# Keys and values of two batches instead of one behind the last expert tile

## The chip, the cores and the metric

The kernel runs on one core of a Trainium2 chip, as one program. A core has TensorE (matmuls), VectorE, ScalarE and GpSimd for everything elementwise, SyncE, which mostly starts transfers, and 16 DMA engines that all of them share. The metric is the device time of one execution in microseconds (us); lower is better. It is given as the median of several runs.

## The reference

The input x has 8 batches of 512 tokens with 256 channels, the context as many. Four residual steps follow each other:

```python
x = x + _L0_xattn_ref(_layernorm(x), ctx, ctx, ...)      # gated attention without softmax
x = x + _L0_ffn_ref(_layernorm(x), Ws, bs, W1, b1, W2, b2)
x = x + _L1_xattn_ref(_layernorm(x), ctx, ctx, mask, Wq, Wk, Wv, Wo)
x = x + _L1_ffn_ref(x, ...)                              # self attention, then top-2 experts
```

The second step is a mixture of experts in which each of 8 experts takes the 512 tokens with the highest router probability:

```python
route_prob = softmax(xf @ Ws + bs).T
route_vals, routes = top_k(route_prob, k)                # k = N / E = 512
h = gelu(einsum('ekd,edf->ekf', xf[routes], W1) + b1)
out = (einsum('ekf,efd->ekd', h, W2) + b2) * route_vals
final = zeros.at[routes].add(out)
```

The third step, a cross attention with 16 heads of 16 channels, needs `k = key @ Wk.T` and `v = value @ Wv.T`, where key and value are both the context. They do not depend on x, so they can be computed at any time before it. This case is about when.

## The kernel before, in words

The program is a row of blocks. In each block every engine has its own instruction stream, written out in program order; engines meet by semaphores, and at the end of a block by a barrier: each engine issues a DRAIN (which ends when its own work is over) and reports to GpSimd, and GpSimd lets all of them go when all have reported and its own DRAIN is over. In the rows below those instructions bear the line at which the block ends: 861 for the search block, 1365 for an experts' block, 1979 for the attention.

The blocks are: `aft_keys`, `aft_tokens` (first attention, router), `expert_choice` (here called the search block), `experts` for the first layer (the experts' block), `attention` (cross and self attention), `experts` for the second.

The **search block** finds, for each of 8 experts, the 512th highest probability by 15 rounds of bits. In a round VectorE compares and TensorE counts. Then token lists of the first two experts are made: VectorE builds one-hot slabs, TensorE sums them (line 701), VectorE enters the list, and GpSimd fetches the tokens' rows by eight indirect gathers (line 711, tile `early_xg`). TensorE is mostly free in this block, so the cross attention's keys and values are projected there, in units put between the rounds. A batch has four units:

```python
if q == 0: self.keys(pe, b, 0)
if q == 1: self.keys(pe, b, 1); self.take_off(pe, b, 0, 0, K0)
if q == 2: self.values(pe, b, 0); self.take_off(pe, b, 1, 0, K1); self.take_off(pe, b, 0, 1, MID0)
if q == 3: self.values(pe, b, 1); self.take_off(pe, b, 1, 1, MID1)
```

`keys` (line 754) and `values` (line 772) are fp32 matmuls. The keys are kept as three bf16 parts: ScalarE copies a bank out as bf16, `take_off` (line 761) subtracts that part in the bank by a matmul with minus one times the identity, and ScalarE copies the rest, twice. So a batch has eight ScalarE copies (`copy_batch`, lines 802 to 818). SyncE stores three parts of keys to `kstack` (line 823, 256 KB each) and the values to `values` (line 829, 574 KB), and loads the context of the batch after next (line 159). Batches count from 0 to 7; batch b uses buffer b % 2.

After the fourth list sum of the search block TensorE runs the units that are left: the last one of batch 5 and all of batch 6 before, with `B - LATE = 7` batches in this block.

The **experts' block** runs 8 tiles of 512 tokens. In a tile TensorE multiplies by W1 (line 1549), ScalarE applies the activation (line 1591), TensorE turns the next tile's rows (line 1537) and multiplies by W2 (line 1571), VectorE adds the bias and scales (lines 1699, 1703), and GpSimd adds the result to the tensor `sum` by indirect transfers with accumulation (line 1495), one at a time. Behind the last tile TensorE projects the batches that are left (batch 7 before), in the banks `exL_pt` and `exL_ph`. SyncE's stream there is:

```python
for b in range(B - LATE, B):
    kv.store_part(sp, G, b, 0, K1)
    kv.store_part(sp, G, b, 1, MID1)
    kv.store_values(sp, G, b)
    if b == B - 1:
        sp.wait_ge(added, begins(tiles) * 16)
        opening.load_rows(sp, G)
    kv.store_part(sp, G, b, 2, LO1)
```

`opening.load_rows` (line 1248) loads the first batch of the new x from `sum` once all scatter-adds are over. VectorE then takes its statistics (lines 370, 373), GpSimd makes the reciprocal spread (lines 380, 381), VectorE normalizes (line 386, tile `open_xn`), and the block ends. The attention starts with TensorE turning `open_xn` (line 2093).

Of the kernel before, what the change touches and what calls it, by code (L numbers as in the profile page):

```python
# [728 lines left out]
FIRST = 2  # L729
K0, K1, MID0, V0, MID1, LO0, V1, LO1 = range(8)  # L730
EVENTS = 8
LATE = 1


class KeyValues:
# [96 lines left out]
def expert_choice(nc, G, a, early, source):  # L832
# [4 lines left out]
    with ExitStack() as ctx:  # L837
# [16 lines left out]
            "vchain", "counted", "totalled", "flagged", "scanned", "ranked", "built", "summed"))  # L854
        kv = KeyValues(st, early, source, pk, pv, 0, B - LATE)
        entered, copied, masked = (st.sem(n) for n in ("entered", "copied", "masked"))
# [4 lines left out]
        with nc.Block() as block:  # L861

            @block.sync
            def _(sp):
                st.set_semaphores(sp)
                early.st.set_semaphores(sp)
                st.retire(sp, G["aft_sems"])
                st.retire(sp, G["tok_sems"])

                def load_expert(e):  # L870
                    sp.dma_start(early.w1[e][:], a["L0_W1"][e].rearrange("(c p) f -> p c f", p=P)).then_inc(early.w1_in[e], 16)
                    sp.dma_start(early.b1[e][:], a["L0_b1"][e]).then_inc(early.w1_in[e], 16)
                    sp.dma_start(early.w2[e][:], a["L0_W2"][e].rearrange("(c p) d -> p c d", p=P)).then_inc(early.w2_in[e], 16)
                    sp.dma_start(early.b2[e][:], a["L0_b2"][e:e + 1, :].broadcast_to([P, D])).then_inc(early.w2_in[e], 16)

                for e in range(FIRST):
                    load_expert(e)

                for b in range(B - LATE):
# [3 lines that stand above are left out]
                    if b + 2 < B:  # L883
                        source.load(sp, a, b + 2)
                    kv.store_part(sp, G, b, 2, LO1)

            @block.scalar
            def _(act):
                act.copy(onesb[:], G["ones"][:]).then_inc(copied, 1)
                act.activation(minus[:], G["identb"][:], ACT.Copy, scale=-1.0).then_inc(copied, 1)  # L890
                for b in range(B - LATE):
                    kv.copy_batch(act, b)
# [111 lines left out]
            def _(pe):  # L1004
                left = iter(range(4 * (B - LATE)))

# [263 lines left out]
def experts(nc, G, a, tag, gelu, early=None, out=None, opening=None, source=None):  # L1270
# [7 lines left out]
    with ExitStack() as ctx:  # L1278
# [32 lines left out]
        if early:  # L1311
            kv = KeyValues(st, early, source, pt, ph, B - LATE, B)
        names = ("turned", "xgT_ready", "hid_ps", "hid_ready", "out_ps", "ys_ready", "put_ready", "biased")
# [51 lines left out]
        with nc.Block() as block:  # L1365

            @block.sync
            def _(sp):
# [24 lines left out]
                if early:  # L1393
                    opening.st.set_semaphores(sp)
                    run(sp, load, 2)
                    opening.load_weights(sp, a)
                    for b in range(B - LATE, B):
                        kv.store_part(sp, G, b, 0, K1)
# [1434 lines left out]
```

## Time and profile before

| | |
|---|---|
| median of 3 runs | 2377.77 us (2376.32 to 2379.54) |
| profiled execution, its own time | 2372.58 us |
| span in that profile | 2370.4 us |
| mean granted TensorE clock | 0.963 |
| TensorE busy | 2177.3 us (92%) |
| VectorE busy | 1339.2 us (56%) |
| ScalarE busy | 1005.1 us (42%) |
| GpSimd busy | 661.2 us (28%) |

The profile is of one execution; its times count from the start of the span. Busy time leaves out DMA-issuing, semaphore and branch instructions. PE is TensorE, PEld its weight loads, DVE VectorE, ACT ScalarE, POOL GpSimd, SP SyncE; a q behind the name (POOLq, SPq) is that engine's sequencer, with DMA issues, waits and DRAINs. The search block lies at 187 to 270 us, the experts' block at 270 to 542 us.

### The profile page before, as it was taken

Reading aid. Unit: us, or ns where it says so; the run is one execution under the profiler, and the core shown is the slowest. Engines: PE = TensorE matmul, PEld = TensorE weight load, DVE = VectorE, ACT = ScalarE, POOL = GpSimd, SP = SyncE. Lnnn points to the kernel's source line nnn. Section 1 sums busy time; section 2 is a strip of 40 time slices with the busy share of each in tenths; the row PEclk is TensorE's granted clock in tenths of the full one; section 3 lists DMA queues with packets and bytes.
Section 4 is the critical chain, followed back from the end, with each engine's and each line's share of the span. In section 5 each row is a group of like instructions: output and inputs, shape, how many; then the busy total and the mean of one; then the engine's idle time right before and its main releaser. Section 6 shows DMA issues by size and latency. Waiting matters only on the chain. (4 is left out here: it accounts for less than half of the span.)

```text
span 2370.4 us, 33096 instructions
## 1 busy us (share of the span) xinstructions
PE 2177.3 (92%) x10807; PEld 1230.4 (52%) x10807; DVE 1339.2 (56%) x3625; ACT 1005.1 (42%) x1823; POOL 661.2 (28%) x671
## 2 busy tenths in 40 slices
PE   6898899985999999999999999999858999999995
PEld 2474566661333433334334343334337888888884
DVE  5556533214777777777777777877854541112125
ACT  2223322110656665665666656666512222222223
POOL 3210233333111001111124233344122343334343
PEclk9998999995999999999999999999968999999997
DMA  5426434435333332321343342443106666667684
GB/s 175 136 98 200 140 97 104 117 70 99 72 66 68 60 69 33 73 51 26 44 55 55 46 55 42 60 64 48 26 31 186 190 186 188 188 189 208 198 274 127
DMA packets 197559, 249.75 MB, mean 105 GB/s; under 512 B 26080, under 2 KB 175584, under 8 KB 195360
## 3 DMA queue, kind: packets, MB, share of 16 engines
q1 hardware_dynamic: 175808, 217.95, 36.6%
q0 software_dynamic: 20736, 29.15, 7.1%
q10 hardware_dynamic: 864, 0.79, 0.3%
q8 instruction: 77, 1.26, 0.2%
q14 instruction: 74, 0.61, 0.1%
HBM read 162.77 MB, written 46.52 MB: 88 GB/s over the span
## 5 line engine op out<-in xcount | busy, mean ns | idle before, releaser
L2343 ACT ACTIVATE att_prob<-att_ps 128x512 f32<-128x512 f32 x1024 | 594.5, 597 | 388.1 <-PE att_ps L2187 200.5
L2477 DVE CUSTOM_DVE_ANT_0 att_junk<-att_pm,bias 128x512 bf16<-128x512 f32 x512 | 343.6, 688 | 166.6 <-PE att_pm L2170 165.3
L2170 PE MATMUL att_pm<-att_kstack,att_qstack 96*128 96x512 bf16 x1024 | 399.4, 391 | 29.1 <-DMA att_qstack<-att_q 24.5
L2473 DVE TENSOR_REDUCE att_tops<-att_pm 128x1 f32<-128x512 f32 x512 | 340.1, 682 | 114.3 <-PE att_pm L2170 112.3
L2184 PE MATMUL att_ps<-att_qstack,att_kstack 99*128 99x512 bf16 x1024 | 390.7, 383 | 9.2 <-DMA att_qstack<-att_negT 4.9
L1591 ACT ACTIVATE exL_hid<-exL_ph,exL_b 128x256 f32<-128x256 f32 (+1 forms) x312 | 144.3, 463 | 390.6 <-PE exL_ph L1549 389.5
L1495 POOL DMA_INDIRECT sum<-exL_ys,exL_put x106 | 176.3, 1663 | 405.9 <-DVE exL_ys L1703 229.6
L1549 PE MATMUL exL_ph<-exL_xgT,exL_w 128*128 128x256 f32 (+1 forms) x1248 | 271.9, 375 | 8.3 <-issue 4.4
L2201 PE MATMUL att_po<-att_prob,att_vals 128*32 128x512 f32 x2048 | 275.4, 610 | 1.0 <-ACT att_prob L2343 1.0
L1571 PE MATMUL exL_po<-exL_w,exL_hid 128*128 128x256 f32 x1184 | 265.4, 382 | 6.0 <-ACT exL_hid L1591 4.0
L2170 PEld LDWEIGHTS att_pm<-att_kstack,att_qstack 96*128 96x128 bf16 x1024 | 100.9, 99 | 300.3 <-DVE att_tops L2477 99.3
L1549 PEld LDWEIGHTS exL_ph<-exL_xgT,exL_w 128*128 128x128 f32 x1248 | 221.3, 192 | 53.7 <-ACT exL_hid L1591 10.9
L1571 PEld LDWEIGHTS exL_po<-exL_w,exL_hid 128*128 128x128 f32 x1184 | 221.8, 190 | 42.7 <-ACT exL_hid L1591 9.8
L2187 PE MATMUL att_ps<-bias,identb 128*128 128x512 bf16 x512 | 194.8, 380 | 0.0
L2184 PEld LDWEIGHTS att_ps<-att_qstack,att_kstack 99*128 99x128 bf16 x1024 | 100.0, 98 | 149.8 <-ACT att_prob L2343 80.5
L1645 DVE COPY exL_xgT<-exL_pt 128x256 f32<-128x256 f32 (+2 forms) x96 | 40.0, 458 | 221.6 <-PE exL_pt L1537 221.4
L380 POOL TENSOR_SCALAR open_rstd<-open_mv 128x4 f32<-128x4 f32 x16 | 3.7, 229 | 495.3 <-DVE open_mv L2450 486.1
L1699 DVE TENSOR_TENSOR exL_ys<-exL_po,exL_b 128x256 f32<-128x256 f32 x74 | 31.4, 424 | 188.0 <-PE exL_po L1571 184.0
L1571 PE MATMUL exL_po<-early_w,exL_hid 128*128 128x256 f32 x512 | 113.6, 381 | 8.6 <-DVE exL_ys L1703 8.6
L1549 PE MATMUL exL_ph<-exL_xgT,early_w 128*128 128x512 f32 x256 | 115.0, 604 | 1.5 <-DVE exL_xgT L1645 1.5
L1591 ACT ACTIVATE exL_hid<-exL_ph,early_b 128x512 f32<-128x512 f32 x64 | 44.0, 687 | 153.6 <-PE exL_ph L1549 153.6
L1571 PEld LDWEIGHTS exL_po<-early_w,exL_hid 128*128 128x128 f32 x512 | 96.2, 190 | 23.8 <-DVE exL_ys L1703 11.1
(415 smaller groups left out, 2614.9 us busy)
## 6 DMA issues: line engine op xcount, KB each, us to landing
exL_w<-in_L_W SPq DMA_DIRECT2D x78, 1024.0 KB, 5.4
att_qstack<-att_q SPq DMA_DIRECT2D x186, 128.0 KB, 5.7
early_w<-in_L_W SPq DMA_DIRECT2D x16, 1024.0 KB, 5.4
att_kstack<-att_k SPq DMA_DIRECT2D x96, 128.0 KB, 4.6
att_kstack<-kstack SPq DMA_DIRECT2D x32, 256.0 KB, 5.0
kstack<-early_k SPq DMA_DIRECT2D x24, 256.0 KB, 4.2
exL_b<-in_L_b SPq DMA_DIRECT2D x39, 128.0 KB, 5.5
values<-early_vals SPq DMA_DIRECT2D x8, 574.0 KB, 3.7
```

Of the source, the lines that this page charges most:

```text
L1495: pool.indirect_dma_start(out=sums[0], out_offset=bass.IndirectOffsetOnAxis(ap=put[slot][:, c:c + 1], axis=0), in_=ys[slot][:, c, :], in_o ...
L1549: mm = pe.matmul(ph[f % 2][:, 0:n * P], w1[slot][:, m, f * P:(f + 1) * P], xgT[:, m, 0:n * P], start=m == 0, stop=m == DC - 1)
L1571: mm = pe.matmul(po[c % 2][:], hid[:, f, c * P:(c + 1) * P], w2[slot][:, f, :], start=f == 0, stop=f == FC - 1)
L1591: act.activation(hid[:, f, 0:n * P], ph[f % 2][:, 0:n * P], gelu, bias=b1[slot][:, f:f + 1]).then_inc(hid_ready, 1)
L1645: ins = dve.tensor_copy(xgT[:, m, 0:n * P], pt[m][:, 0:n * P])
L2170: pe.matmul(pm[i % TOPS][:], stack["q"][par][0:KR, h, t * P:(t + 1) * P], stack["k"][par][0:KR, h, :], start=True, stop=True).then_inc(s[" ...
L2184: mm = pe.matmul(ps[i % 2][:], stack["k"][par][0:KR + 3, h, kc * P:(kc + 1) * P], stack["q"][par][0:KR + 3, h, :], start=True, stop=me.self_)
L2187: mm = pe.matmul(ps[i % 2][:], G["identb"][:], G["bias"][1][:, kc, :], start=False, stop=True)
L2201: mm = pe.matmul(po[j * 32:j * 32 + 32, :], vals[par][:, kc, h * VW:h * VW + 32], prob[(i + j) % PROBS][:], start=kc == 0, stop=kc == CB - 1)
L2343: act.activation(prob[i % PROBS][:], ps[i % 2][:], ACT.Exp, scale=SCALE).then_inc(s["p_ready"], 1)
L2473: ins = dve.tensor_reduce(tops[g % 2][:, t, j:j + 1], pm[i % TOPS][:], AX.X, ALU.max)
L2477: ins = dve.tensor_tensor_reduce(junk[:, i % TOPS, :], pm[i % TOPS][:], G["bias"][0][:, t, :], 1.0, -BIG / 2, ALU.add, ALU.max, tops[g % 2 ...
```

## The change

The number of batches whose keys and values are projected behind the last expert tile goes from one to two. Every loop that splits the batches between the two blocks reads it, on TensorE (units), ScalarE (copies) and SyncE (stores); VectorE and GpSimd keep their streams.

```diff
 FIRST = 2
 K0, K1, MID0, V0, MID1, LO0, V1, LO1 = range(8)
 EVENTS = 8
-LATE = 1
+LATE = 2
```

On TensorE, at the end of the search block. `pick_pk` and `pick_pv` are the banks of keys and values; `early_k` are the saved bf16 parts.

```order
 L772 MATMUL pick_pv<-source_wv,source_src 128x256 x4
 L761 MATMUL pick_pk<-early_k,early_minus 128x512
-L754 MATMUL pick_pk<-source_src,source_wk 128x512 x4
-L761 MATMUL pick_pk<-early_k,early_minus 128x512
-L772 MATMUL pick_pv<-source_wv,source_src 128x256 x4
-L761 MATMUL pick_pk<-early_k,early_minus 128x512 x2
-L772 MATMUL pick_pv<-source_wv,source_src 128x256 x4
-L761 MATMUL pick_pk<-early_k,early_minus 128x512
 L861 UNCONDITIONAL_BRANCH
```

Batch 6 is gone from there: behind batch 5's last values comes the end of the block. At the end of the experts' block the same six rows are put between the last tile's line 1571 and batch 7, in the banks `exL_pt` and `exL_ph`.

On SyncE, at the end of the search block and at the end of the experts' block.

```order
 L829 DMA values<-early_vals 128x1148
 L159 DMA source_src<-in_ctxT 128x2x512
-L823 DMA kstack<-early_k 128x2x512 x3
-L829 DMA values<-early_vals 128x1148
 L823 DMA kstack<-early_k 128x2x512
 L861 UNCONDITIONAL_BRANCH
```

```order
 L823 DMA kstack<-early_k 128x2x512 x2
 L829 DMA values<-early_vals 128x1148
+L823 DMA kstack<-early_k 128x2x512 x3
+L829 DMA values<-early_vals 128x1148
 L1248 DMA x<-sum 128x4x256
 L823 DMA kstack<-early_k 128x2x512
```

Four stores left the first place and stand in the second, ahead of the load of x at line 1248. The context loads of line 159 all stay in the search block. On ScalarE the eight copies of lines 802 to 818 move in the same way. The order of GpSimd's and VectorE's instructions is the same in both kernels.

## Rows read from the trace of the kernel before

**Rows 1.** Timeline of PE, 258 to 275: start, us, engine, what, idle before.

```profile
259.14 0.38 PE L761 MATMUL pick_pk<-early_k,early_minus 128*128 128x512 bf16 x1
...
266.89 0.38 PE L761 MATMUL pick_pk<-early_k,early_minus 128*128 128x512 bf16 x1
270.21 1.35 PE L1537 MATMUL exL_pt<-ident,early_xg 128*128 128x128 f32 x8 [2.94 <-PEq L861]
```

**Rows 2.** Line 861, end of the search block: count, ns min/median/max, first and last start.

```profile
L861 POOLq EVENT_SEMAPHORE  x2: 17/17/17, 270.0 to 270.0; - x2
L861 POOLq DRAIN  x1: 10547/10547/10547, 259.4 to 259.4; - x1
...
L861 SPq DRAIN  x1: 122/122/122, 268.6 to 268.6; - x1
```

**Rows 3.** Timeline of POOL, 255 to 270.

```profile
263.54 0.95 POOL L711 DMA_INDIRECT early_xg<-rows,early_get  x1 [0.30 <-issue]
```

**Rows 4.** Timeline of POOL, 520 to 545.

```profile
535.36 1.05 POOL L381 TENSOR_TENSOR open_rstd<-open_rstd,mhalf 128x4 f32<-128x4 f32 x1
```

**Rows 5.** Line 1365, end of the experts' block, 520 to 545.

```profile
L1365 POOLq DRAIN  x1: 6397/6397/6397, 535.3 to 535.3; - x1
L1365 DVEq DRAIN  x1: 1295/1295/1295, 536.7 to 536.7; - x1
```

**Rows 6.** End of the attention: line 1979, and POOL's last instruction.

```profile
L1979 POOLq DRAIN  x1: 2452/2452/2452, 1760.5 to 1760.5; - x1
...
1760.55 2.35 POOL L2407 TENSOR_TENSOR x<-x,att_yn 128x1024 f32<-128x1024 f32 x1
```

**Rows 7.** Timeline of PE, 518 to 552.

```profile
526.49 0.38 PE L761 MATMUL exL_pt<-early_k,early_minus 128*128 128x512 bf16 x1
542.18 1.09 PE L2093 MATMUL att_pja<-ident,open_xn 128*128 128x128 f32 x4 [15.30 <-PEq L1365]
```

**Rows 8.** Timeline of ACT, 518 to 545.

```profile
526.69 0.59 ACT L816 COPY early_vals<-exL_ph 128x512 f32<-128x512 f32 x1 [0.59 <-PE exL_ph L772]
```

**Rows 9.** Timeline of SP, 518 to 534.

```profile
527.31 0.33 SPq L829 DMA_DIRECT2D values<-early_vals  x1
528.42 0.36 SPq L1248 DMA_DIRECT2D x<-sum  x1
```

**Rows 10.** Waits of SP, 520 to 545: total us, times, longest.

```profile
SPq L1365 <- PEq L1365: 8.0, 1, 8.0
...
SPq L1248 <- DMA sum<-exL_ys,exL_put: 0.8, 1, 0.8
```

**Rows 11.** Timeline of DVE, 518 to 542.

```profile
532.97 1.40 DVE L370 BATCH_NORM_STATS2 open_stats<-x 128x6 f32<-128x256 f32 x4 [12.92 <-DMA x<-sum]
...
536.51 1.38 DVE L386 TENSOR_SCALAR open_xn<-x,open_mv,open_rstd 128x256 f32<-128x256 f32 x4 [1.73 <-POOL open_rstd L381]
```

**Rows 12.** Stretches: busy us of each engine, PEclk, DMA share, GB/s.

```profile
core 0: us, PE busy (x) PEld busy (x) DVE busy (x) ACT busy (x) POOL busy (x), PEclk, DMA share, GB/s
188.00:192.00 4.00, 3.83 (x5) 1.77 (x6) 1.47 (x6) 0.01 (x1) 1.11 (x3) 0.50 0.00 0
192.00:196.00 4.00, 4.00 (x17) 2.44 (x17) 1.25 (x6) 1.65 (x3) 0.00 (x0) 0.96 0.78 266
263.00:267.00 4.00, 4.00 (x20) 3.14 (x18) 0.00 (x0) 2.62 (x5) 1.18 (x2) 1.00 1.02 341
273.00:277.00 4.00, 3.98 (x5) 1.85 (x6) 3.70 (x8) 0.17 (x1) 0.00 (x0) 0.50 0.00 0
277.00:281.00 4.00, 4.00 (x10) 1.64 (x9) 2.56 (x7) 1.44 (x3) 0.00 (x0) 0.92 0.02 4
534.00:542.00 8.00, 0.00 (x0) 0.00 (x0) 2.13 (x10) 0.00 (x0) 1.31 (x3) 0.50 0.00 0
```

**Rows 13.** Issue to landing: load of x (L1248), then the context loads (L159) at 225:270.

```profile
DMA to landing us min/median/max: 4.5/4.5/4.5
...
DMA to landing us min/median/max: 5.1/5.2/6.9
```

## The prediction

> **What bounds the kernel now.** I read in this order: the busy line of the table above, each engine's timeline around the two places that the constant touches, the lines on which a block of the program ends, SyncE's waits, and the granted clock in short stretches. TensorE is busy for 92% of the span, but one batch of keys and values is a few us of it; what counts is which wait ends last at the end of the search block (line 861) and at the end of the first experts' block (line 1365).
>
> The search block. TensorE ends batch 5 at 259.14 + 0.38 = 259.52, batch 6 at 266.89 + 0.38 = 267.27, and then has nothing until 270.21 [rows 1]. Batch 6 is therefore 267.27 - 259.52 = 7.75 us of TensorE. Who holds the block until 270.0? Every engine ends it with a DRAIN. TensorE's work is over at 267.27, SyncE's DRAIN at 268.6 + 0.12 = 268.7, and GpSimd's lasts from 259.4 for 10.547 us, to 269.9; its two semaphore events, which let all engines go, stand at 270.0 [rows 2]. GpSimd's last instruction, the eighth gather of token rows, was over at 263.54 + 0.95 = 264.49 [rows 3]. So its drain goes on for 5.4 us behind its last instruction, and outlasts SyncE by 1.2 us.
>
> The experts' block shows the same. GpSimd's last instruction ends at 535.36 + 1.05 = 536.41 [rows 4], its drain at 535.3 + 6.40 = 541.7, that of VectorE at 536.7 + 1.30 = 538.0 [rows 5]: 5.3 us behind GpSimd's last instruction and 3.7 us behind VectorE. This is also no matter of traffic, since the DMA share from 534 to 542 is 0.00 [rows 12]. In the block of the attention, where GpSimd issues no indirect DMA, its last instruction ends at 1760.55 + 2.35 = 1762.90 and its drain at 1760.5 + 2.45, together with it [rows 6]. The reader is to see a fixed tail of 5.3 to 5.4 us, counted from GpSimd's own last instruction, in the two blocks that this change touches.
>
> Behind the last tile TensorE projects batch 7 until 526.49 + 0.38 = 526.87 and then idles for 15.30 us [rows 7]. In that gap runs a chain. ScalarE saves the second half of the values (526.69, 0.59) [rows 8]; SyncE stores them at 527.31, waits for the last scatter-add, and loads the first rows of x at 528.42 [rows 9], a wait of 0.8 us [rows 10]; VectorE's statistics start when they have landed, at 532.97, after 12.92 us of idling, and its last pass starts at 536.51 when GpSimd has given the spread [rows 11]; then come the 5.3 us of drain. Attention's first transposes start at 542.18 [rows 7].
>
> **The front: what the removal gives.** It takes the matmuls of batch 6, 7.75 us, from TensorE, eight copies from ScalarE and four stores (three of 256 KB, one of 574 KB) from SyncE, all behind the last thing that GpSimd needs: the fourth list sum of the block. GpSimd's and VectorE's streams are the same, so the eighth gather still ends at 264.49 and the drain still ends 5.3 to 5.4 us later. What I take away was under that cover: gain 0 us, at most 0.1 from the drain being 5.3 and not 5.4. If the drain were not fixed and fell with the stores, the block could end as soon as the last gather is issued: 270.0 - 264.5 = 5.5 us. That end I keep for a rival.
>
> It also has a cost. TensorE now idles from 259.52 to 270.2, 10.7 us and not 2.9. Before, the clock is at 0.50 from 273 to 277 and at 0.92 from 277 to 281 [rows 12], so it came back at about 277.6, and the eight transposes at 270.21 took 1.35 us, most of them still at full clock [rows 1]. After the 15.3 us of idling at the other place, four such transposes took 1.09 [rows 7], so eight take about 1.09 x 2 = 2.2, less the pipelined overlap, some 1.9: +0.55 us, in front of VectorE's copy and the first tile's matmuls. When the clock comes back after that is open from both sides. At the search block's begin TensorE was busy for 3.83 us of 188 to 192, that is from 188.2, at 0.50, and had 0.96 over 192 to 196, so full clock from about 192.3, 4.2 us after the restart [rows 12]; counted so from 270.2 it would be back at 274.4, 3.2 us earlier than before, worth 1.6 us of work at double speed. Before it took 7.4 us from that restart (270.2 to 277.6), for TensorE stood idle between the transposes and the first long matmuls, as it will again; and if it returned as much later as it can earlier, 1.6 us would be lost. I take 0 for it, and +0.5 for the term (range -1.1 to +2.2).
>
> A rule of the Trainium skill speaks against this change here: the page "TensorE: Matmul & The Clock Gate", section "Part 1: The HAM clock gate", has the array fall to 1.2 GHz once it has been idle and return to 2.4 GHz after sustained work. By that rule the transposes start slow, as the row after 15.3 us of idling shows; without it the term would be 0 and the sum 7.3.
>
> **The back: what the addition costs.** The same 7.75 us of matmuls, eight copies and four stores now stand ahead of batch 7, in the block whose end had TensorE idle for 15.3 us. Idle as TensorE is there, the work is not free, because x's load stands in SyncE's queue behind the store of batch 7's values, and this waits for their copy. Batches follow each other without a stall: the banks and buffers that batch 7's first keys need were saved by then, as in the search block, where batch 6 followed batch 5 at once. All of batch 7 moves by 7.75 us: its values are stored at 527.31 + 7.75 = 535.06. The last scatter-add does not move (it hangs on the last tile alone and is over at 528.4), so the 0.8 us wait is gone, and what was hidden in it is all the cover there is. The store takes SyncE 0.33 us [rows 9], so x's load is issued at 535.4, which is 7.0 us later than 528.42.
>
> Then the landing. Before it took 4.5 us, issued 1.1 us behind the 574 KB of values; in the search block a load of the same 512 KB, issued right behind such a store, took 5.1 to 6.9, median 5.2 [rows 13]. With 4.5 VectorE starts 7.0 us later, with 5.2 it is 7.7. The truth lies between and I take 7.3. Batch 6's own stores are no queue in front of it: 1.34 MB per 7.75 us, against the 341 GB/s that 263 to 267 shows [rows 12], are done in half that time. Behind the landing nothing changes: statistics, spread, last pass and drain hang on each other. SyncE stood 8.0 us at the barrier [rows 10], and its last store moves by at most 7.75 with the barrier, so it stays 8 us early. The next stage's loads and clock start from the same gap of some 15 us of idling, so I give them nothing.
>
> On the load the skill has a rule in "Trainium Kernel Development and Optimization", section "Key Constraints": DMAs of all queues share the same 16 engines and interleave. By it the load pays for values' bytes still under way and lands nearer to the 5.2; with queues independent of one another it would be 4.5. Sum 7.7 or 7.0.
>
> **Sum.** Front: 0 gained, +0.5 lost at the clock. Back: +7.3. Together +7.8 us. The profiled execution took 2372.58 us, 2.2 more than its span of 2370.4; with the change it would be 2380.4. The median of the runs is 2377.77, 5.2 above the profiled one, so the predicted median is 2385.6, 0.33% slower. The terms' bounds give +7.0 - 1.1 = 5.9 to +7.7 + 2.2 = 9.9, so 2383.7 to 2387.7.
>
> **Rivals.**
> A. The drain is not fixed. Place: the end of the search block. If GpSimd's drain waits for transfers or for the other engines' traffic, removing batch 6 ends the block up to 5.5 us earlier, and the sum is +7.8 - 5.5 = +2.3, 2380.1 us: not slower by more than a measurement can tell (0.2%, 4.8 us, is the bound for that). It decides as soon as more than 3.0 of the 5.5 us come back. For it: the last gather was still in flight when the drain began, and the stores were too, with a DMA share of 1.02 [rows 12]. Against it: the drain of the second block was as long (5.3) with no byte moving. Chance 0.08.
> B. The back is hidden. If something else than batch 7's values held x's load, the second batch would be free: sum 0.5, 2378.3 us. For it: TensorE's 15 us of idling there, which look like room. Against it: SyncE waits 0.8 us for the scatter-add and no more. It would need a scatter-add that ends 7 us later than in this trace. Chance 0.04.
> C. The clock costs more than I give it: the return to full speed comes a whole step later in the first tile and the landing is at its upper end, +9.9 us, 2387.7. Same sign as the forecast. Chance 0.12.
> D. A real gain, by an effect that I do not see. Chance 0.02. My forecast keeps 0.74.
>
> From these: slower by over 0.2% has 0.74 + 0.12 = 0.86, less 0.01 for a forecast that falls just under the bound: 0.85; within 0.2%: A, B and that, 0.13; faster 0.02. The range takes in the terms' bounds and 1 us to each side for the spread of medians (the three runs span 3.2 us): 2382.6 to 2388.6. It leaves out A and B.
>
> **What would show it.** In the profile after: the search block's GpSimd drain ends again at about 269.9 with SyncE's now before 262; no batch 6 in that block, TensorE idle for 10.7 us; the eight transposes at 1.8 to 2.0 us; 15.6 us of projections behind the last tile; the wait for the scatter-add gone from SyncE's waits; x's load issued about 7 us later against the last scatter-add, and attention's first transpose some 7.8 us later than 542.18. I am wrong if the drain ends before 268 (A), if x's load is issued before 530 (B), or if the first tile's matmuls run at half clock beyond 281 (C).

## The result and the profile after

The change makes the kernel slower: 2385.27 us against 2377.77 us, medians of 7 runs each, ratio 1.003 with a 95% interval of 1.0017 to 1.0043. 1.003 is 7.1 us, the interval 4.0 to 10.2 us. The forecast was +7.8 us, to 2385.6. The profiled execution took 2385.27 us, its span 2383.1 us, mean granted clock 0.96.

The end of the search block comes first: the rows of line 861, then GpSimd's last gather in its timeline, then what the rows of line 711 give for its landing (microseconds from the start of the instruction to its last byte).

```profile
L861 POOLq EVENT_SEMAPHORE  x2: 17/17/17, 271.8 to 271.9; - x2
...
L861 POOLq DRAIN  x1: 8726/8726/8726, 263.0 to 263.0; - x1
...
L861 SPq DRAIN  x1: 123/123/123, 265.4 to 265.4; - x1
```

```profile
267.21 0.95 POOL L711 DMA_INDIRECT early_xg<-rows,early_get  x1 [0.30 <-issue]
```

```profile
DMA to landing us min/median/max: 4.2/4.2/4.2
```

The same line of before, for its last gather:

```profile
DMA to landing us min/median/max: 6.0/6.0/6.0
```

The last gather is issued until 267.21 + 0.95 = 268.16 and the drain ends at 263.0 + 8.73 = 271.7: 3.6 us behind it, where before it was 5.4 [rows 2, 3]. The step that called this tail fixed is wrong. That all of it stands 3.7 us later in the span than before is not the change's work: executions differ by some microseconds ahead of this place (the last gather ends at 263.4 to 268.6 us in the fourteen traces of this study, 263.5 and 263.6 in the second ones of before and after). Hence I measure pieces from the last gather's end on.

TensorE at both places, after:

```profile
262.79 0.38 PE L761 MATMUL pick_pk<-early_k,early_minus 128*128 128x512 bf16 x1
272.04 1.94 PE L1537 MATMUL exL_pt<-ident,early_xg 128*128 128x128 f32 x8 [8.87 <-PEq L861]
...
520.49 3.60 PE L754 MATMUL exL_pt<-source_src,source_wk 128*128 128x512 f32 x8
...
535.78 0.38 PE L761 MATMUL exL_pt<-early_k,early_minus 128*128 128x512 bf16 x1
551.53 1.09 PE L2093 MATMUL att_pja<-ident,open_xn 128*128 128x128 f32 x4 [15.38 <-PEq L1365]
```

TensorE idles for 8.87 us in front of the eight transposes, and they take 1.94 us instead of 1.35 [rows 1]. Windows of the clock behind them. The columns are those of [rows 12]; the granted clock is the figure ahead of the last two, and 0.50 is the lower of its two levels:

```profile
273.00:277.00 4.00, 2.54 (x7) 1.42 (x6) 2.98 (x3) 1.28 (x1) 0.00 (x0) 0.50 0.01 4
277.00:281.00 4.00, 4.00 (x9) 1.75 (x8) 3.70 (x8) 1.09 (x2) 0.00 (x0) 0.83 0.00 0
```

A mean of 0.83 over the second window, from 0.50 and 1.00, puts the return to full clock at 278.4, 6.3 us behind the first transpose (before: 277.6, 7.4 us behind it [rows 1, 12]).

At the back, projections run from 520.49 to 536.16, twice as long. SyncE's timeline and then its waits from 520 to 553 (total us, times, longest):

```profile
528.84 0.33 SPq L829 DMA_DIRECT2D values<-early_vals  x1
529.33 5.95 SPq L823 DMA_DIRECT2D kstack<-early_k  x3
536.59 0.33 SPq L829 DMA_DIRECT2D values<-early_vals  x1
536.97 0.43 SPq L1248 DMA_DIRECT2D x<-sum  x1
```

```profile
SPq L1365 <- PEq L1365: 8.0, 1, 8.0
...
SPq L829 <- ACT early_vals L816: 2.6, 2, 1.3
```

The wait of line 1248 for the scatter-add [rows 10] is gone. x's load is issued 536.97 - 520.49 = 16.5 us behind the first key matmul; before it was 9.5. GpSimd's and VectorE's part, GpSimd's drain, and the landing of x's load:

```profile
525.72 1.55 POOL L1495 DMA_INDIRECT sum<-exL_ys,exL_put  x1 [2.92 <-DMA sum<-exL_ys,exL_put]
544.72 1.04 POOL L381 TENSOR_TENSOR open_rstd<-open_rstd,mhalf 128x4 f32<-128x4 f32 x1
```

```profile
542.32 1.41 DVE L370 BATCH_NORM_STATS2 open_stats<-x 128x6 f32<-128x256 f32 x4 [20.75 <-DMA x<-sum]
```

```profile
L1365 POOLq DRAIN  x2: 5269/5832/6394, 544.7 to 2375.2; - x2
```

```profile
DMA to landing us min/median/max: 5.3/5.3/5.3
```

The last scatter-add was over at 529.5 (3.8 us from its start, by the records of its semaphore); the load stands 7.4 us behind that. In before it stood right behind it, at 528.42 [rows 9, 10]. The line of GpSimd's drain holds two of them, and the block's is the one of 6394 ns. It ends at 544.7 + 6.39 = 551.1, again 5.3 us behind GpSimd's last instruction [rows 4, 5].

The pieces of each profile, in us. "Tail" is GpSimd's drain at line 861 behind the end of the last gather; "middle" goes from that gather to the first key matmul behind the last tile, "last" from there to the attention's first transpose. "Slow until" is how long after the first of the eight transposes the clock was back at 1.0.

| kernel | tail | transposes | slow until | middle | last | middle + last |
|---|---|---|---|---|---|---|
| before | 5.44 | 1.35 | 7.4 | 254.5 | 23.2 | 277.7 |
| before, again | 4.54 | 1.07 | 8.3 | 253.8 | 23.9 | 277.7 |
| after | 3.60 | 1.94 | 6.3 | 252.3 | 31.0 | 283.4 |
| after, again | 3.60 | 1.94 | 9.2 | 253.7 | 31.0 | 284.8 |

Middle less tail is 249.0 and 249.2 us before, 248.7 and 250.1 after: beyond the drain it is the clock that moves middle, up or down with "slow until".

Taken in pairs, middle moves by -2.1 and -0.1 us and last by +7.8 and +7.2: +5.7 and +7.1 in sum, beside the +7.1 us that the runs measured.

### The profile page after: what moved, and what is told of

Same layout as the page of the kernel before. It is cut to its first block and busy times, and to the rows that moved or that the text cites. A ratio compares the mean times of both kernels' runs of the same rounds, so it can differ in the third digit from the quotient of the medians.

```text
span 2383.1 us, 33096 instructions
## 1 busy us (share of the span) xinstructions
PE 2182.2 (92%) x10807; PEld 1232.8 (52%) x10807; DVE 1340.1 (56%) x3625; ACT 1004.7 (42%) x1823; POOL 659.0 (28%) x671
```

## The experiments

All times are medians, in brackets the median of the kernel before beside it on the same chip; ratios have 95% intervals. The theory after the result: the back costs what was forecast, by x's load; at the front the drain waits for something that batch 6 delays, and the clock takes most of it back.

### Front alone

The experts' block projects batch 7 only. Batch 6 is not projected at all; four stores put other data in its place.

```diff
-for b in range(B - LATE, B):                 # SyncE, ScalarE; units on TensorE
+store the four tiles of buffer 0 to the places of batch 6
+for b in range(B - 1, B):
```

> The front half of the change alone: batch 6 is projected in neither block; its four stores send what its buffers hold from batch 4, at the begin of the experts' block, and only batch 7 follows the last tile. Three pieces are read in its trace: the tail of GpSimd's drain at line 861 behind the end of the last gather (5.44 us before, 3.60 after), the stretch from the end of that gather to the first key matmul behind the last tile (254.5 before, 252.3 after), and the stretch from there to the attention's first transpose (23.2 before, 31.0 after). My theory now: the drain ends when the last gather has landed, and batch 6's stores delayed that landing. So tail 3.5 to 3.7, middle stretch 252.3 give or take 1.5 for the clock, last stretch 23.2; faster than before by about 2 us, ratio 0.999. The rival that I forecast from, a fixed drain: tail 5.4, middle 254.5 plus 0.5, time as before plus 0.5 us.

Measured: 2377.41 us (2378.51), ratio 1.000 [0.9988, 1.0011]. Line 861, and TensorE's timeline:

```profile
L861 POOLq DRAIN  x1: 8650/8650/8650, 259.3 to 259.3; - x1
```

```profile
268.20 1.94 PE L1541 MATMUL exL_pt<-ident,early_xg 128*128 128x128 f32 x8 [9.01 <-PEq L861]
...
541.55 1.09 PE L2097 MATMUL att_pja<-ident,open_xn 128*128 128x128 f32 x4 [15.51 <-PEq L1365]
```

Tail 3.54, transposes 1.94, full clock only 9.3 us behind them, middle 253.75, last 23.4. So the drain does give 1 to 2 us back, and the slow clock takes most of it in this profile: middle and last together are 277.2 and not 277.7. The runs, with an interval of some 2.7 us to either side, could not show a gain of that size.

### Back alone

The search block stays as before, and the experts' block projects batches 6 and 7, so batch 6 is projected twice. Told against the kernel after, without the semaphore counts that go with it:

```diff
-LATE = 2
+LATE = 1
-for b in range(B - LATE, B):                 # experts' block, all three engines
+for b in range(B - 2, B):
```

> The back half alone: the search block as before with batch 6 in it, and batch 6 projected and stored a second time behind the last tile, ahead of batch 7. My theory: tail 5.4 and middle stretch 254.5 as before, last stretch 31.0 and not 23.2, so slower than before by 7.8 us, ratio 1.0033. With the front's part of the theory, this is 2 us slower than the changed kernel. The rival, that the front gives nothing: as slow as the changed kernel, less 0.5 us.

Measured: 2382.15 us (2378.51), ratio 1.0018 [1.0009, 1.0028]. SyncE and TensorE:

```profile
534.34 0.33 SPq L829 DMA_DIRECT2D values<-early_vals  x1
534.72 0.43 SPq L1248 DMA_DIRECT2D x<-sum  x1
```

```profile
549.25 1.09 PE L2093 MATMUL att_pja<-ident,open_xn 128*128 128x128 f32 x4 [15.34 <-PEq L1365]
```

Last 31.0, as in after to 0.04 us, tail 5.38: the back is all in this part. But 7.7 us of pieces stand beside 1.0018, 4.3 us, at most 6.7. It was run again:

> The back half alone once more, since its first timing (ratio 1.0018, 1.0009 to 1.0028, some 4.3 us) lies under what its trace shows (7.7 us in the pieces that differ). If that was chance of the timing: ratio 1.0025 to 1.004 now, last stretch 31.0 again. If it is real: 1.0018 again, and something behind the last stretch gives back 3 us whenever only the back half is changed.

Measured: 2382.83 us (2376.83), ratio 1.0027 [1.0015, 1.0039], that is +6.4 us, 3.6 to 9.3; tail 5.54, last 31.0. The second interval holds the 7.7 us, the first one does not. The profile's places do not differ between the two, so I take the first as a low draw, which is argued and not shown.

### What holds the drain: batch 6's stores moved away

The kernel before, with batch 6's four stores at the experts' block's begin. Matmuls and copies stay in the search block.

```diff
-for b in range(B - LATE):                    # SyncE, search block
+for b in range(B - 2):
+# experts' block, ahead of batch 7: the four stores of batch 6
```

> The kernel before with one edit: batch 6 is still projected and copied in the search block, but its four stores are issued at the begin of the experts' block. TensorE and ScalarE do there all that they did before. My theory, that the stores' traffic delays the last gather's landing and with it the drain: tail 3.5 to 3.7, last stretch 23.2, and the middle stretch shorter than before by 1.8 to 2.5 us, as TensorE has idled no longer than 5 us when the tile begins. Ratio 0.999. Rival one, a fixed drain: tail 5.4, time as before. Rival two, that it is the work of TensorE and ScalarE on the on-chip memory that holds GpSimd, and not the stores: tail 5.4 as well, which then contradicts e1 if that one has 3.6.

Measured: 2377.23 us (2378.51), ratio 0.9998 [0.9987, 1.0009]. Line 861, and the landing of the last gather:

```profile
L861 POOLq DRAIN  x1: 9813/9813/9813, 258.5 to 258.5; - x1
```

```profile
DMA to landing us min/median/max: 5.3/5.3/5.3
```

Tail 4.70, between before's 5.44 and after's 3.6; middle is 253.9, not the 1.8 us or more below 254.5 that was expected. The 5.3 us of landing go with it: the gather was issued at 262.69, 262.69 + 5.28 = 268.0, and the drain ended at 268.3. From these three tails the stores look like part of it and not all; but the second profile of before, further down, has 4.54 with all its stores in place, so this run alone does not show what they do. In all fourteen traces GpSimd's drain at line 861 ends 0.37 or 0.38 us after the last gather's last byte (read from the records of its semaphore): 6.0 us of landing and 5.4 of tail before, 4.2 and 3.6 after. The drain waits for GpSimd's own gathers; what varies is how long these take. The landing is what the tail was all the time, and it equalled the other block's 5.3 by chance.

### Stores alone, copies alone

After, with batch 6's place taken once by four stores (of batch 4's buffers), once by eight ScalarE copies (of a key bank, with no projection):

```diff
+# SyncE, search block, behind batch 5's: 3 stores of keys, 1 of values
```

```diff
+# ScalarE, search block, behind batch 5's: 2 x (3 casts of pk[1], 1 copy of pk[1])
```

> The changed kernel, and in its search block SyncE also issues batch 6's four stores, with what their buffers hold from batch 4, right behind batch 5's; they are sent again with batch 6's values behind the last tile. No copy and no matmul of batch 6 is in the search block. It asks what delays the last gather's landing, with which GpSimd's drain ends in every trace (0.38 us behind it). So far: 3.1 to 3.4 us behind the last gather without anything of batch 6 or with TensorE's work alone; 4.3 with matmuls and copies but no stores; 4.2, 5.0 and 5.1 with all three. If the stores do it: landing 4 us or more, tail 4.4 or more. If the copies do it: tail 3.5 to 3.7.

> The changed kernel, and in its search block ScalarE runs eight more copies of a bank into batch 6's buffers behind batch 5's, back to back; no store and no matmul of batch 6 there. If ScalarE's copies delay the last gather: tail 4.4 to 4.8. If not: 3.5 to 3.7, and then the stretch with matmuls and copies but no stores (4.7) needs both together.

One profile each: 2389.66 us and 2384.53 us (2376.83). Stores alone, line 861 and SyncE:

```profile
L861 POOLq DRAIN  x1: 10702/10702/10702, 261.1 to 261.1; - x1
```

```profile
263.49 2.37 SPq L887 DMA_DIRECT2D kstack<-early_k  x3
265.90 0.94 SPq L889 DMA_DIRECT2D values<-early_vals  x1
```

Copies alone, line 861 and ScalarE:

```profile
L861 POOLq DRAIN  x1: 9761/9761/9761, 259.4 to 259.4; - x1
```

```profile
260.36 1.58 ACT L898 CAST early_k<-pick_pk 128x512 bf16<-128x512 f32 x3
...
263.70 0.69 ACT L899 COPY early_vals<-pick_pk 128x512 f32<-128x512 f32 x1
```

Tails 5.59 and 4.64, where the seven traces with neither have 3.4 to 3.7: the stores alone bring all of before's first profile, the copies alone bring the 1.1 us that the kernel with late stores still had. The two do not add up. The stores are issued earlier here than in before, from 1.8 us ahead of the last gather, where before's come from 0.06 us behind its start on; so this shows that stores can do it, not how much before's own do. That they delay a landing fits shared DMA engines. One execution each says nothing of a microsecond of time.

For the copies the traces hold a rival that no run tests. In all six in which batch 6's copies, or eight like them, are in the search block (both profiles of before, both of back alone, late stores, copies alone) a DMA packet of 8 KB of the kind "instruction" starts 2.2 to 2.8 us ahead of the last gather; in the eight others none starts between 17 us ahead of that gather and 6 us behind its start. In the DMA view of before, 255 to 262 us:

```profile
q14 instruction: 1, 0.01, 0.7%
```

In copies alone 9 of the gather's 144 packets, one sixteenth, end one after the other from 3.95 to 4.74 us behind its start; after's are all over at 3.7. The context load issued 3.2 us ahead of the gather lands 1.1 us later too. So one of the 16 DMA engines seems to have been held up, and a packet of ScalarE's longer code, and not the copying, may be the cause. Which of the two it is stays open.

### x's load ahead of batch 7's stores

After, with SyncE's order changed.

```diff
 for b in range(B - LATE, B):
+    if b == B - 1:
+        sp.wait_ge(added, begins(tiles) * 16)
+        opening.load_rows(sp, G)
     kv.store_part(sp, G, b, 0, K1)
     kv.store_part(sp, G, b, 1, MID1)
     kv.store_values(sp, G, b)
-    if b == B - 1:
-        sp.wait_ge(added, begins(tiles) * 16)
-        opening.load_rows(sp, G)
     kv.store_part(sp, G, b, 2, LO1)
```

> The changed kernel with one edit: behind batch 6's stores SyncE waits for the last scatter-add and loads x's first rows before it waits for any part of batch 7. My theory, that the 7.8 us come only from x's load standing behind batch 7's values in SyncE's queue: x's load is issued as soon as the scatter-add is over, 9.5 us behind the first key matmul and not 16.5, the last stretch is 23.2 to 23.7 and not 31.0, and the kernel is faster than the one before by about 2 us, ratio 0.999. The rival, that TensorE's and ScalarE's second batch is itself what the barrier waits for: last stretch still near 31. A third way, that batch 7's stores now share the DMA engines with x's load: 24 to 25.

Measured: 2375.05 us (2378.51), ratio 0.9989 [0.998, 0.9999]. SyncE, then TensorE:

```profile
528.54 0.36 SPq L823 DMA_DIRECT2D kstack<-early_k  x1
528.95 1.30 SPq L1248 DMA_DIRECT2D x<-sum  x1
531.71 2.79 SPq L823 DMA_DIRECT2D kstack<-early_k  x2
535.81 0.33 SPq L829 DMA_DIRECT2D values<-early_vals  x1
```

```profile
544.14 1.09 PE L2093 MATMUL att_pja<-ident,open_xn 128*128 128x128 f32 x4 [8.77 <-PEq L1365]
```

The projections are the same 15.7 us, and last falls from 31.0 to 24.4: 6.6 us of the back's cost are x's place in the queue, not the work. Statistics start 6.0 us after the issue instead of 4.5 [rows 9, 11], the load now following batch 6's last stores closely; in the next kernel, with the same order, it was 4.5, and last 23.5. By pieces this kernel is at +0.8 against before, by the runs at -2.6 (-4.8 to -0.2); that gap of 3.4 us is not explained by any row.

### Before and after once more

> The kernel before itself, unchanged, timed against itself and profiled once more. The reason: the three traces so far that share a piece agree in that piece to 0.1 or 0.2 us, but the profiled execution of before (2372.6) lies 5.9 us under its own median (2378.5), and what is left outside the pieces that the change touches differs by 2 to 4 us from trace to trace. Expected: ratio 1.000 give or take 0.001; drain tail 5.4 us, middle stretch 254.4 to 254.5, last stretch 23.2 to 23.4 again; the time ahead of the last gather and the time behind the attention's first transpose other than in the first trace by 1 to 4 us. If instead those two stretches repeat to 0.3 us, they are not chance, and the gap between the sums of the pieces and the medians needs another cause.

> The changed kernel once more beside it. Expected: tail 3.5 to 3.7, middle stretch between 252.3 (half clock until 9.5 us behind the last gather, as in its first trace) and 253.8 (half clock for one step longer, as in the front-only kernel), last stretch 31.0. The pieces add up to +5.7 to +7.2 us against before, ratio 1.0024 to 1.0030. The rival, my forecast of +7.8 with no gain at the front, ratio 1.0033.

Measured: before 2376.98 us (2377.58), ratio 1.000 [0.9989, 1.001]; after 2383.44 us (2377.58), ratio 1.0034 [1.0021, 1.0047], +8.0 us. Line 861 of each:

```profile
L861 POOLq DRAIN  x1: 9647/9647/9647, 258.4 to 258.4; - x1
```

```profile
L861 POOLq DRAIN  x1: 8717/8717/8717, 258.5 to 258.5; - x1
```

The unchanged before shows a tail of 4.54 and transposes of 1.07. So the tail moves by 0.9 us with no change at all, after's stays at 3.60, and the gain at the drain is 0.9 to 1.8 us. The two of back alone, whose search block is before's, have 5.38 and 5.54: four tails of 4.5 to 5.5 against five of 3.5 to 3.7 (after twice, front alone, x's load first, and the spread moved, below), 1.6 us between the means. After's middle is 252.3 and 253.7; the 1.4 us between its two profiles lie in the clock, back 6.3 us behind the first transpose in one, 9.2 in the other.

### TensorE kept at work while the drain lasts

The previous kernel (load first) and, at the end of TensorE's search block, eight more matmuls (whose result nobody reads) on a weight and a context tile that are already there.

```diff
+pe.wait_ge(kv.kv_saved, kv.event(B - LATE - 1, LO1))
+pe.wait_ge(source.src_in[0], past(4 * 16))
+for _ in range(8):
+    pe.matmul(pk[0][:], source.wk[:, 0, 0:P], source.src[0][:, 0, :], start=True, stop=True)
```

> The kernel with x's load first, and behind batch 5's last copy in the search block TensorE runs 8 more fp32 matmuls of 512 columns whose results nobody reads, some 7 us, so that it idles 2 to 4 us and not 9 to 10 before the experts' block. No stores and no copies are added. My theory on the middle stretch, that what the shorter drain gave was mostly eaten by the clock: the eight transposes take 1.1 to 1.4 us and not 1.94, half clock ends as in before or earlier, and the stretch is 252.0 to 253.0 against 254.05, so 1 to 2 us faster than that kernel. The rival, that the stretch is longer for another reason: 254 again. It also tells what held the last gather in the kernel with late stores, where the tail was 4.7 and not 3.6: if TensorE's work alone does it, the tail here is about 4.7; if ScalarE's copies or chance, 3.6.

Measured: 2374.89 us (2377.58), ratio 0.9988 [0.9978, 0.9999]. TensorE (each of these fp32 matmuls stands as two records), and the clock from 273 to 277:

```profile
259.99 7.13 PE L1045 MATMUL pick_pk<-source_src,source_wk 128*128 128x512 f32 x16 [1.16 <-ACT early_k L818]
267.83 1.07 PE L1541 MATMUL exL_pt<-ident,early_xg 128*128 128x128 f32 x8 [0.71 <-PEq L861]
```

```profile
273.00:277.00 4.00, 4.00 (x10) 1.82 (x9) 3.72 (x12) 1.37 (x2) 0.00 (x0) 0.91 0.00 0
```

Transposes 1.07, clock back 5.9 us behind the first of them, middle 251.6 against 254.05 of the kernel without the eight matmuls, 2.4 us less. But the five traces with this search block and no such matmuls spread from 252.3 to 254.1 (mean 253.2), so the gain is 0.7 to 2.4 us, 1.6 in the mean. The tail is 3.54, so a busy TensorE does not lengthen the gather's landing. The runs do not tell this kernel from the previous one (0.9989), each measured against before.

### The spread without GpSimd

Load first, and the reciprocal spread made by VectorE (add, reciprocal) and ScalarE (square root) instead of GpSimd, so that GpSimd's last work in the block is the scatter-add.

```diff
-opening.scale_of(pool, G)
+dve.tensor_scalar(rstd, variance, EPS, None, ALU.add)
+act.activation(warm, ones, ACT.Sqrt)         # loads the table ahead of time
+act.activation(rstd, rstd, ACT.Sqrt)
+dve.reciprocal(rstd, rstd)
```

> The kernel with x's load first, and the reciprocal spread of the opening made by VectorE (sum, reciprocal) and ScalarE (square root) in place of GpSimd's power. GpSimd's last work in the experts' block is then the last scatter-add. In all traces its drain there ends 5.3 us behind its last instruction although its last transfer landed 13 us before. My theory, that this is a fixed time counted from its last instruction: the drain then ends near or before VectorE's last pass, the block ends with VectorE, and the last stretch is 3 to 3.6 us shorter than the 24.4 of the kernel with the load first, so 20.8 to 21.5; ratio to before 0.9975. The rival, that the drain waits for all other engines or ends only when the block does: 24.4 again.

Measured: 2373.8 us (2377.58), ratio 0.9985 [0.9974, 0.9996]. GpSimd; the block's end (each line holds two drains, and this block's is the longer one, that starts first); TensorE:

```profile
526.44 1.55 POOL L1509 DMA_INDIRECT sum<-exL_ys,exL_put  x1 [3.01 <-DMA sum<-exL_ys,exL_put]
```

```profile
L1379 POOLq DRAIN  x2: 5258/6127/6996, 526.5 to 2355.2; - x2
...
L1379 DVEq DRAIN  x2: 730/1010/1291, 539.5 to 2359.0; - x2
```

```profile
541.29 0.68 PE L2109 MATMUL att_pja<-ident,open_xn 128*128 128x128 f32 x4 [4.71 <-PEq L1379]
```

Now the block ends with VectorE, at 539.5 + 1.29 = 540.8, and last is 20.4, 4.1 us less than with load first, 3.2 less than in the second kernel of that order (23.5). SyncE, which waits at the block's end for batch 7's stores to land, is done only 0.06 us ahead of VectorE (540.78 and 540.84 us), so those stores nearly hold the block now. The runs give 3.6 us against before (1.0 to 6.2), where 0.9975, 5.9 us, was expected. GpSimd's drain, 526.5 to 533.5, ends 5.5 us behind its last instruction, but long before it matters.

### All three together

> The fastest that I can put together: two batches behind the last tile, x's load ahead of batch 7's stores, the 8 unread matmuls that keep TensorE's clock, and the spread made by VectorE and ScalarE. By the pieces: tail 3.5, transposes 1.07, middle stretch 251.6 (as with the matmuls alone), last stretch 20.4 (as with the spread moved), so 272.0 and not 277.7 from the last gather to the attention: 5.7 us faster than before, ratio 0.9976. The rival, that these gains do not add: no better than the kernel with the spread moved (0.9985).

Measured: 2372.0 us (2376.83), ratio 0.9977 [0.9963, 0.9991], 5.5 us faster than before (2.1 to 8.8). TensorE, then the clock from 270 to 273:

```profile
267.15 1.07 PE L1554 MATMUL exL_pt<-ident,early_xg 128*128 128x128 f32 x8 [0.30 <-PEq L861]
...
533.73 1.09 PE L2113 MATMUL att_pja<-ident,open_xn 128*128 128x128 f32 x4 [4.68 <-PEq L1383]
```

```profile
270.00:273.00 3.00, 3.00 (x8) 1.33 (x7) 2.70 (x8) 0.69 (x1) 0.00 (x0) 1.00 0.00 0
```

No half clock at the block's start, middle 249.95, last 20.3: 7.4 us less than before in pieces. It has the lowest median of the study, but the runs do not tell it from the kernel with the spread moved (0.9985); only the pieces do, 270.3 us against 272.7 for middle and last. Whether it needs the second late batch was not tried. SyncE is again done only 0.06 us ahead of VectorE, where with one late batch it stood at the barrier 8.0 us early [rows 10]; one late batch with the spread moved is what to try next.

## Why the prediction was right, and where it was not

**The back, +7.3: right.** Last went from 23.2 and 23.9 to 31.0, +7.2 to +7.8 (the forecast's bounds were 7.0 and 7.7). Both its parts held: the load issued 7.0 us later against the first key matmul in the first pair of profiles and 6.5 in the second, and the landing took 5.3 us, 0.1 above the forecast's upper end of 5.2 (4.5 and 4.8 before). The values' store and x's load are both SyncE's, so this landing says nothing of how separate queues share. That the place in SyncE's queue causes it is shown by load first (24.4), and that it needs nothing of the front by back alone (31.0).

**The front, gain 0: wrong in its reason.** The step that failed is the "fixed tail of 5.3 to 5.4 us, counted from GpSimd's own last instruction". At line 861 it is the landing of the last gather and 0.4 us; 5.44 and 4.54 in two profiles of before, 3.60 in both of after. It was read from one execution and from the likeness of two places, 5.4 and 5.3, which is no evidence of one cause. A second profile of the same kernel would have refuted it. The sign given for A, a drain that ends before 268, could not: it counts from the start of the span, and by it after stands at 271.8 and 267.2, before at 269.9 and 268.1. The sentence that spoke for rival A, that gather and stores were in flight, was the right one: rival A's mechanism, that the drain waits for transfers, is what the stores alone show. Its size was not: the whole 5.5 us could not come back, since the gather lands 3.2 us behind its instruction's end even without batch 6; 0.9 to 1.8 did, under the 3.0 from which A would have decided.

**The clock, +0.5: right in the mean, and it varies by more than its own size.** The transposes took 1.94 in both profiles of after, "some 1.9" being the forecast; TensorE idled for 8.9 and not 10.7 us. Against the second profile of before, which has 1.07, the term is +0.9. The return to full clock came 1.1 us sooner after the transposes in one pair and 0.9 later in the other, so the 0 taken for it lay in the middle. Middle less tail, which leaves the clock and the tiles, is 249.1 in the mean of the four traces with before's search block (249.0 to 249.2) and 249.6 in the five with after's (248.7 to 250.3): the term measured +0.5. With the eight added matmuls it is 248.1 and 246.6, so by this estimate the kernel before already pays 1.0 to 2.5 us to the clock there, which the change did not bring. The Trainium skill's page "TensorE: Matmul & The Clock Gate", section "Part 1: The HAM clock gate", has the array fall to 1.2 GHz when idle, and the trace agrees: 0.50 over the transposes after 8.9 us of idling, 1.00 after 0.3 us.

**Sum.** Front as forecast +0.5, measured as middle, mean of two against mean of two: 253.0 - 254.1 = -1.1, of which the drain gave -1.4 and the clock took +0.3. So the theory of the experiments, that the clock takes most of the drain's gain back, holds for single profiles and not for the mean. Back +7.3, measured +7.5 by the same means. +6.4 in pieces, beside +7.1 and +8.0 in two measurements. The forecast of +7.8 is 1.4 above the pieces, the drain's share, and within both intervals, which cannot tell 6.4 from 7.8; that the median fell within 0.4 us of 2385.6 is luck, since the stretches ahead of and behind these pieces differ by up to 4.6 and 4.4 us among the four executions.

## What to carry to other kernels

Work put where TensorE idles is free only if nothing in another engine's queue stands behind it: look which transfer waits for its results in program order, and put the load that ends the block ahead of the stores that only the block's end waits for. Where a DRAIN outlasts its engine's last instruction, compare its end with the landing of that engine's own transfers, and in more than one profile of the kernel: at line 861 the two go together, at line 1365 they do not, and tails of one length in two blocks need not have one cause. Time won by a gap in front of a block is in part lost again to the clock; a few unread matmuls in the gap are cheap.

## What the runs showed of the hardware

GpSimd's DRAIN at the end of the search block ended 0.37 or 0.38 us after its last indirect gather had landed, in all fourteen traces. With neither copies nor stores of batch 6 in that block the landing took 3.9 to 4.3 us from the start of the gather (seven traces). With eight more ScalarE copies it took 5.2 and 5.3 (two traces), and an instruction packet of 8 KB stood ahead of it; which of the two delays it is open. With four stores of SyncE's queue (1.34 MB) and no copies it took 6.2 (one trace), with stores and copies 5.1 to 6.1 (four traces).

In the experts' block GpSimd's drain ended 5.3 us behind a GpSimd elementwise instruction that started with the last scatter-add over for 15 us (after). Where the scatter-add itself was the last, it ended 5.5 and 5.3 us behind that, 2.7 us after its landing both times (the kernel with the spread moved, all three together). So it is not true of this block that a DRAIN ends when its engine's own work is over. In the attention's block, without indirect transfers, it was under 0.1 us [rows 6]. What the drain waits for in the experts' block is open; taking GpSimd's last instruction out of the block's last chain, which needs no answer to that, gave 3.2 to 4.1 us.
